# A graph network's setup on one core: the order in which x, the weights and the edge lists are loaded and used

## Chip, core and metric

The kernel runs on one core of one Trainium2 chip. The metric is the device time of one launch in microseconds. The kernel before takes 2194.6 us (median of three runs, 2194.39 to 2196.65).

## What is computed

A two-layer graph attention network over N = 3125 nodes of width 1024 and E = 50000 edges that are sorted by their target node. Each layer is added to its input and normalized. Only the first layer matters here, and of it only what stands ahead of its main products:

```python
xp = (x @ W).reshape(N, H, C)              # N=3125, H=4 heads, C=256, W is 1024 x 1024
a_src = jnp.einsum('nhc,hc->nh', xp, att_src)
a_dst = jnp.einsum('nhc,hc->nh', xp, att_dst)
e = jax.nn.leaky_relu(a_src[src] + a_dst[dst], 0.2)
ee = jnp.exp(e - m[dst])                   # m: the largest e of each target node
alpha = ee / z[dst]                        # z: the sum of ee of each target node
out = jax.ops.segment_sum(xp[src] * alpha[:, :, None], dst, num_segments=N)
x = _layernorm(x + relu(out + bias))       # then the second layer, in the same way
```

The kernel uses that `a_src` and `a_dst` are x times a small matrix, `wa` (1024 x 8): the weights W projected on the attention vectors.

## The kernel before

The change touches the setup, roughly the first 93 us. After it the kernel's first main stage multiplies the transposed x with W on TensorE (the line `L973` of the profile).

The setup is two blocks of hand-written programs, one for each engine, that meet at a barrier. The first block (`order_edges`) tests whether the edges are sorted, copies them, and already issues the loads of the attention vectors and of W (`load_weights`, eight parts of 128 rows, 512 KB each; three count on one semaphore, five on another). The second block has these programs:

- **SP** issues the loads of x. x is 25 tiles of 128 nodes, loaded as 13 pairs (1 MB each, the last is 53 rows). Before, it issues pairs 0 and 1, then one load of the last target of each chunk of 128 edges (`isrc`, 390 words of 4 bytes), then eleven small loads of the edge lists (`wrow` and `lrow`, up to 110 rows of about 512 bytes), and then the other pairs of x.
- **TensorE** transposes each tile of x (eight blocks of 128x128, counted by the profile as 8 or 16 instructions for one or two tiles), and ScalarE copies each tile back from PSUM to SBUF (`evict`). Tiles go in *quads*, quarters of x of four pairs each. When a quad's tiles are all transposed and `wa` is there, `products_a` multiplies the quad with `wa` (`L631`). `sources` transposes tables of the edge chain, `sums(0)` and `sums(1)` transpose the results of the first two and the last two quads (`L648`), and `first_tile` does the first products of the main stage (`L655`). `in_turn` holds this order for TensorE and ScalarE alike. Ahead of one tile TensorE broadcasts a row of 391 words (`s_bcast`) that VectorE's edge chain waits for.
- **VectorE** computes `wa` in eight steps, one for each part of W, each of eight `tensor_tensor_reduce` (the profile's `L692 CUSTOM_DVE_ANT_0` and the reading of its sum). Then comes the *edge chain* (`L701` to `L736`), which makes the table `ct`, the chunk numbers `cii`, and numbers for each block of edges. Then it waits for the gathered table `st` and derives `wrow`, `lrow` and the masks from it (`L746` to `L769`), and last the attention terms of the nodes (`L772` to `L783`).
- **GpSimd** stores `ct` to memory and gathers its rows as `st`.

Of the kernel before, what the change touches and what calls it, by code (L numbers as in the profile page):

```python
# [31 lines left out]
P = 128  # L32
# [276 lines left out]
def gnn_kernel(nc, x, src, dst, w0, att_s, att_d, bias, rms_w, w_down, wl, wr, att1, w_up, out):  # L309
# [22 lines left out]
    with top:  # L332
# [37 lines left out]
        with ExitStack() as ph:  # L370
# [12 lines left out]
            assert 5 * KEYS + EC <= (NT - 1) * D  # L383
# [124 lines left out]
            def in_turn(tile, quad, sources, sums):  # L508
                for t in range(14):
                    tile(t)  # L510
                quad(0)
                tile(14)
                tile(15)
                quad(1)
                for t in range(16, 24):
                    tile(t)
                sources()
                quad(2)
                sums(0)
                tile(24)  # L520
                quad(3)
# [6 lines left out]
            with nc.Block() as block:  # L528
                @block.gpsimd
                def _(pool):  # L530
                    pool.wait_ge(s_ct, 1)
# [10 lines left out]
                def _(sp):  # L542
                    sp.wait_ge(s_pad, 4)
                    load_x(sp, range(2))
                    with nc.allow_non_contiguous_dma(reason="one word of each chunk"):
                        sp.dma_start(lasti[0:1, 0:NCF], dst[0:NCF * P].rearrange("(c k) -> k c", k=P)[P - 1:P, :])\
                          .then_inc(s_lrow, 16)
                    dh = dst.tensor

                    first = sp.dma_start(dx[0:1, 0, 1:P + 2], dst[0:P + 1].rearrange("(a k) -> a k", a=1))  # L550
                    first.then_inc(s_edges, 16)
                    n_edge = 1
                    for b in range(NB):
                        c0, c1 = max(1, b * TB), min((b + 1) * TB, NCF)
                        sp.dma_start(dx[c0 - b * TB:c1 - b * TB, b, :],
                                     bass.AP(dh, c0 * P - 1, [[P, c1 - c0], [1, P + 2]])).then_inc(s_edges, 16)
                        c0 = b * TB
                        sp.dma_start(sx[0:c1 - c0, b, :],
                                     src[c0 * P:c1 * P].rearrange("(p k) -> p k", k=P)).then_inc(s_edges, 16)
                        n_edge += 2  # L560
                    pl, bl = NCF % TB, NCF // TB
                    sp.dma_start(dx[pl:pl + 1, bl, 0:E_LAST + 1],
                                 dst[NCF * P - 1:E].rearrange("(a k) -> a k", a=1)).then_inc(s_edges, 16)
                    sp.dma_start(sx[pl:pl + 1, bl, 0:E_LAST],
                                 src[NCF * P:E].rearrange("(a k) -> a k", a=1)).then_inc(s_edges, 16)
                    assert n_edge + 2 == N_EDGE_DMAS
                    load_x(sp, range(2, NPAIR))
# [9 lines left out]
                def _(act):  # L577
                    def evict(t):
                        act.wait_ge(s_tr, t + 1)
                        r = t % 2  # L580
# [3 lines left out]
                    def take_a(q):  # L584
                        act.wait_ge(s_am, q + 1)
                        n = min(2 * P, (NT - 2 * GROUPS * q) * P)
                        nc.scalar.activation(aT[:, q, 0:n], psum[:, 4 + 2 * (q % 2), 0:n], ACT.Copy).then_inc(s_ac, 1)
# [1710 lines left out]
```

## Time and profile before

| | |
|---|---|
| median of three runs | 2194.6 us |
| the profiled execution: its time, its span | 2195.57 us, 2193.9 us |
| TensorE busy over the span | 1793.3 us, 82% |
| VectorE busy | 1514.8 us, 69% |
| GpSimd, ScalarE busy | 1197.0 us (55%), 996.7 us (45%) |
| end of the setup (VectorE's first instruction of the next block) | 92.87 us |

All rows come from one profiled execution, with times counted from the start of its span. The setup is some 4% of the span (92.87 of 2193.9 us), so shares over the whole span say little about it; the timelines of its engines say more. A timeline row is a start, a duration, the engine, the line of the kernel, what is written from what, and in brackets how long the engine was idle ahead of it and what ended that.

### The profile page before, as it was taken

What the parts mean: (1) busy time and instruction counts of PE and PEld (TensorE: products, weight loads), DVE (VectorE), ACT (ScalarE), POOL (GpSimd) and SP (SyncE); (2) the same over time, 40 slices, a digit from 0 to 9 for tenths busy, and PEclk for the clock granted to TensorE, in tenths of its full rate; (3) what the DMA queues carried; (4) which work ended last, traced back from release to release, by engine and by line L of the source; (5) the groups of instructions that cost most, each with busy time, mean ns of one, the idle gap of its engine ahead of it and who ended that gap; (6) DMA issues with size and microseconds to landing.
All of it is one profiled execution on the core that took longest, in us unless ns stands there. A gap on an engine that the chain in (4) does not pass through costs nothing. (4 is left out here: it accounts for less than half of the span.)

```text
span 2193.9 us, 51575 instructions
## 1 busy us (share of the span) xinstructions
PE 1793.3 (82%) x12059; PEld 1230.1 (56%) x12060; DVE 1514.8 (69%) x3657; ACT 996.7 (45%) x3133; POOL 1197.0 (55%) x1696
## 2 busy tenths in 40 slices
PE   4899999995888888888849896887878878466688
PEld 3555555543666566566638774665666666455543
DVE  6577777747766666666669983555656556888867
ACT  3200000024777777777747662332333333466566
POOL 1122222223777777777711116777777776588780
PEclk9999999997999999999979998999999999699999
DMA  8345443313999999999999965887879877988757
GB/s 329 114 109 106 106 106 107 101 45 119 362 357 352 361 358 353 358 357 353 360 271 319 306 204 161 246 242 216 251 229 246 247 223 226 286 311 310 270 193 261
DMA packets 254648, 539.12 MB, mean 246 GB/s; under 512 B 40301, under 2 KB 146422, under 8 KB 254510
## 3 DMA queue, kind: packets, MB, share of 16 engines
q0 software_dynamic: 87696, 275.50, 36.5%
q1 hardware_dynamic: 72670, 175.70, 25.6%
q10 hardware_dynamic: 94176, 86.66, 13.7%
q8 instruction: 47, 0.77, 0.1%
q14 instruction: 59, 0.48, 0.1%
HBM read 448.51 MB, written 102.18 MB: 251 GB/s over the span
## 5 line engine op out<-in xcount | busy, mean ns | idle before, releaser
L1248 ACT ACTIVATE wone<-onehot,w 128x64 f32<-128x64 f32 x1760 | 432.3, 333 | 149.5 <-DVE onehot L1294 144.1
L161 POOL DMA_INDIRECT acc<-xl_table,csrc x392 | 395.0, 1008 | 128.0 <-issue 114.6
L1265 PE MATMUL banks<-w_sb,wone 128*64 128x256 f32 x2368 | 318.5, 395 | 77.6 <-DMA w_sb<-xp_table,isrc 46.8
L161 POOL DMA_INDIRECT w_sb<-xp_table,isrc x296 | 296.9, 1003 | 90.5 <-issue 57.0
L973 PE MATMUL banks<-w_sb,acc 128*128 128x512 f32 x736 | 342.5, 604 | 0.0
L1290 DVE TENSOR_TENSOR acc<-banks,acc 128x512 f32 x440 | 304.4, 692 | 0.0
L1737 PE MATMUL banks<-acc,onehot_t 128*128 x880 | 231.8, 408 | 82.5 <-ACT onehot_t L1712 56.9
L1765 DVE SCALAR_TENSOR_TENSOR prod<-banks,att_relu 128x1024 f32<-128x1024 f32 x110 | 134.7, 1225 | 205.7 <-ACT w L1702 205.7
L1737 PEld LDWEIGHTS banks<-acc,onehot_t 128*128 128x128 f32 x880 | 163.2, 195 | 146.2 <-issue 122.6
L1742 PE MATMUL banks<-acc,ident 128*128 x880 | 217.5, 391 | 24.6 <-POOL tabs L1664 24.5
L1265 PEld LDWEIGHTS banks<-w_sb,wone 128*64 128x64 f32 x2368 | 163.2, 138 | 127.1 <-issue 42.7
L1708 ACT ACTIVATE away<-lt,edge 128x512 f32<-128x512 bf16 x110 | 79.4, 722 | 296.8 <-issue 152.3
L1742 PEld LDWEIGHTS banks<-acc,ident 128*128 128x128 f32 x880 | 167.0, 193 | 64.0 <-issue 38.6
L973 PEld LDWEIGHTS banks<-w_sb,acc 128*128 128x128 f32 x736 | 131.2, 191 | 122.1 <-issue 122.0
L1289 DVE TENSOR_TENSOR zacc<-banks,zacc 64x9 f32 x440 | 69.8, 159 | 187.4 <-PE banks L1268 169.0
L863 POOL COPY w<-at_dst 128x16 f32 (+1 forms) x110 | 30.7, 279 | 308.0 <-DVE w L1071 268.0
L1878 POOL TENSOR_TENSOR scan_buf<-rows,w 128x1536 f32<-128x1536 f32 x55 | 151.7, 2777 | 49.6 <-PE banks L1918 32.5
L1918 PE MATMUL banks<-scan_buf 128*64 128x132 f32 x1760 | 126.4, 286 | 62.8 <-DVE acc L1947 33.4
L1265 PE MATMUL banks<-rows_c,wone 128*64 128x256 f32 x1152 | 153.4, 390 | 27.1 <-DMA rows_c<-xp_table,isrc 14.1
L161 POOL DMA_INDIRECT rows_c<-xp_table,isrc x144 | 144.3, 1002 | 43.9 <-issue 26.2
L909 ACT ACTIVATE zacc<-pidx 128x450 f32<-128x450 f32 x1 | 0.6, 577 | 361.9 <-DVE onehot_t L1059 361.9
L1268 PEld LDWEIGHTS banks<-w,onehot 128*64 128x64 f32 x880 | 121.3, 138 | 64.9 <-issue 1.9
(340 smaller groups left out, 2936.4 us busy)
## 6 DMA issues: line engine op xcount, KB each, us to landing
edge_rows<-acc ACTq DMA_DIRECT2D x440, 130.0 KB
rows<-edge_rows SPq DMA_DIRECT2D x55, 1040.0 KB, 5.0
lt_bc<-local_dst ACTq DMA_DIRECT2D x110, 128.0 KB, 3.6
lt<-local_dst SPq DMA_DIRECT2D x110, 128.0 KB, 4.3
w<-acc SPq DMA_DIRECT2D x100, 128.0 KB, 3.5
x_table<-y POOLq DMA_DIRECT2D x25, 512.0 KB, 5.9
acc<-x_table SPq DMA_DIRECT2D x25, 512.0 KB, 3.6
low_bc<-src_low ACTq DMA_DIRECT2D x98, 128.0 KB, 4.1
```

The costliest lines, as they stand in the source:

```text
L161: return self.pool.indirect_dma_start(out, None, table, bass.IndirectOffsetOnAxis(ap=idx, axis=0), bounds_check=self.bound, oob_is_err=False)
L973: last = nc.tensor.matmul(psum[:, 2 * r + i], xT_all[:, u, k, :], w_sb[:, k, i * 512:(i + 1) * 512], start=(k == 0), stop=(k == KD - 1))
L1248: last = nc.scalar.activation(wone[:, s, j, h, :], onehot[:, s, j, :], ACT.Copy, scale=w9[:, bass.ds(g * U + j, 1), h:h + 1].rearrange("p ...
L1265: nc.tensor.matmul(psum[WN * a:WN * (a + 1), j, k * C:(k + 1) * C], wone[:, s, j, h, :], slots[r][:, j, h * C:(h + 1) * C], start=True, st ...
L1268: nc.tensor.matmul(psum[0:WN, 4 + j, 0:W9], onehot[:, s, j, :], w9[:, bass.ds(i, 1), :].rearrange("p a n -> p (a n)"), start=True, stop=Tr ...
L1290: nc.vector.tensor_tensor(av, psum[:, j, :], av, ALU.add).then_inc(s_acc, 1)
L1708: nc.scalar.activation(away[:], lt[:, s].rearrange("p j e -> p (j e)"), ACT.Abs, bias=edge[:, 0:1]).then_inc(s_ab, 1)
L1737: nc.tensor.matmul(psum[:, 4 * s2 + j, 0:XRW], onehot_t[:, s2, j, :], xr[:, bass.ds(ds[j], 1), :].rearrange("p a n -> p (a n)"), start=Tru ...
L1742: last = nc.tensor.matmul(psum[:, 4 * s2 + j, 0:XLW], ident[:], rows[:, bass.ds(ss[j], 1), :].rearrange("p a n -> p (a n)"), start=False, ...
L1765: nc.vector.scalar_tensor_tensor(out=prod[:, s], in0=psum[:, 4 * s:4 * s + 4, 0:HID], scalar=0.0, in1=bc(att_relu[:].unsqueeze(1), [P, U, ...
L1878: nc.gpsimd.tensor_tensor(msg[:, s, :, 0:POOL_HEADS, 0:HD], rows[:, r, :, 0:POOL_HEADS * HD].rearrange("p j (h c) -> p j h c", c=HD), bc(w ...
L1918: last = nc.tensor.matmul(psum[WN * a:WN * (a + 1), bank, c:c + 2 * HS], onehot[:, u, first + j, :], msg[:, s, j, 2 * a:2 * a + 2, :].rear ...
```

## The change

Four things change, all in the setup:

1. The quads go in the order third, first, second, fourth (`QUAD_ORDER`), and the tiles with them (`TILE_ORDER`: 16 to 23, 0 to 15, 24). Pairs 8 and 9, half of the third quad, are loaded ahead of W, in `load_weights`; the other eleven loads of x follow in the second block without a break.
2. The load of `isrc` and the eleven edge loads are issued by GpSimd instead of SP, at the start of the second block.
3. VectorE does its edge chain between the third and the fourth part of W, and signals that `wa` is ready (`s_wa`) after the fifth to eighth.
4. TensorE transposes twenty tiles and does `sources` ahead of the first quad's products; the broadcast stands ahead of the ninth tile (`BCAST = 8`), not ahead of the eleventh.

```diff
-            assert 5 * KEYS + EC <= (NT - 1) * D
+            EARLY, BCAST = 2, 8
+            QUAD_ORDER = [EARLY, *(q for q in range(len(QUADS)) if q != EARLY)]
+            TILE_ORDER = [t for q in QUAD_ORDER for p in QUADS[q] for t in (2 * p, 2 * p + 1) if t < NT]
+            place_of = {t: i for i, t in enumerate(TILE_ORDER)}
+            turn_of = {q: i for i, q in enumerate(QUAD_ORDER)}
...
             def load_weights(sp):
                 sp.dma_start(attd, att_d.rearrange("h c -> (h c)").partition_broadcast(P)).then_inc(s_att, 16)
+                load_x(sp, QUADS[EARLY][:2])
                 for k in range(KD):
...
             def in_turn(tile, quad, sources, sums):
-                for t in range(14):
-                    tile(t)
-                quad(0)
-                tile(14)
-                tile(15)
-                quad(1)
-                for t in range(16, 24):
+                for t in TILE_ORDER[:20]:
                     tile(t)
                 sources()
-                quad(2)
+                quad(QUAD_ORDER[0])
+                for t in TILE_ORDER[20:24]:
+                    tile(t)
+                quad(QUAD_ORDER[1])
+                quad(QUAD_ORDER[2])
                 sums(0)
-                tile(24)
-                quad(3)
+                tile(TILE_ORDER[24])
+                quad(QUAD_ORDER[3])
                 sums(1)
...
                 @block.gpsimd
                 def _(pool):
+                    pool.wait_ge(s_pad, 4)
+                        pool.dma_start(lasti[0:1, 0:NCF], dst[0:NCF * P].rearrange("(c k) -> k c", k=P)[P - 1:P, :])\
+                          .then_inc(s_lrow, 16)
...
+                    for b in range(NB):
+                        c0, c1 = max(1, b * TB), min((b + 1) * TB, NCF)
+                        pool.dma_start(dx[c0 - b * TB:c1 - b * TB, b, :],
+                                     bass.AP(dh, c0 * P - 1, [[P, c1 - c0], [1, P + 2]])).then_inc(s_edges, 16)
...
                     pool.wait_ge(s_ct, 1)
...
                 @block.sync
                 def _(sp):
                     sp.wait_ge(s_pad, 4)
-                    load_x(sp, range(2))
...
-                        sp.dma_start(lasti[0:1, 0:NCF], dst[0:NCF * P].rearrange("(c k) -> k c", k=P)[P - 1:P, :])\
-                          .then_inc(s_lrow, 16)
...
-                    load_x(sp, range(2, NPAIR))
+                    load_x(sp, [p for q in QUAD_ORDER for p in QUADS[q]][2:])
...
                     def transposes(t):
                         pe.wait_ge(s_xi[t // 2], 16)
-                        wait(pe, s_xT, t - 1)
-                        if t == 10:
+                        i = place_of[t]
+                        wait(pe, s_xT, i - 1)
+                        if i == BCAST:
                             pe.wait_ge(s_lastw, 1)
...
                     def sums(i):
                         pe.wait_ge(s_csrc, 1)
-                        pe.wait_ge(s_ac, min(2 * i + 2, len(QUADS)))
+                        pe.wait_ge(s_ac, 1 + max(turn_of[2 * i], turn_of[2 * i + 1]))
...
                 @block.vector
-                    for k in range(KD):
+                    def project(k):
                         dve.wait_ge(s_w[k >= W_FIRST], 16 * (KD - W_FIRST if k >= W_FIRST else W_FIRST))
-                        if k == W_FIRST:
-                            dve.wait_ge(s_iota, 11)
-                            dve.wait_ge(s_lrow, 16)
-                            link(nc.vector.tensor_copy(lastf, lasti))
-                            nc.vector.tensor_tensor(lastw, lastf, iotc, ALU.add).then_inc(s_lastw, 1)
...
-                    nc.vector.tensor_copy(mark0[:], pidx[:]).then_inc(s_wa, 1)
+                    for k in range(W_FIRST):
+                        project(k)
+                    dve.wait_ge(s_iota, 11)
+                    dve.wait_ge(s_lrow, 16)
+                    link(nc.vector.tensor_copy(lastf, lasti))
+                    nc.vector.tensor_tensor(lastw, lastf, iotc, ALU.add).then_inc(s_lastw, 1)
 
                     dve.wait_ge(s_edges, 16 * N_EDGE_DMAS)
                     link(nc.vector.tensor_copy(dxf, dx))
...
                     link(nc.vector.scalar_tensor_tensor(out=toff[:], in0=toff[:], scalar=float(WN), in1=dneg[:],
                                                         op0=ALU.mult, op1=ALU.add))
+
+                    for k in range(W_FIRST, KD):
+                        project(k)
+                    nc.vector.tensor_copy(mark0[:], pidx[:]).then_inc(s_wa, 1)
```

The program of TensorE from its first transpose of the setup, before (`acc` is x, `nt` is `wa`, `isfirst` is the row that is broadcast, `ct` and `val` are the edge tables of `sources`):

```order
L618 MATMUL banks<-ident,acc 128x128 x80
L615 MATMUL banks<-isfirst,any_b 110x391
L618 MATMUL banks<-ident,acc 128x128 x32
L631 MATMUL banks<-acc,nt 32x256 x32
L618 MATMUL banks<-ident,acc 128x128 x16
L631 MATMUL banks<-acc,nt 32x256 x32
L618 MATMUL banks<-ident,acc 128x128 x64
L639 MATMUL banks<-ident,ct 128x110
```

And now:

```order
L623 MATMUL banks<-ident,acc 128x128 x64
L620 MATMUL banks<-isfirst,any_b 110x391
L623 MATMUL banks<-ident,acc 128x128 x96
L644 MATMUL banks<-ident,ct 128x110
L645 MATMUL banks<-ident,val 128x110
```

Both quads' products that stood ahead of `sources` have left this piece; twenty tiles (160 transposes) stand there.

The same engine from the last transpose of `sources` on, before (the `w` of `L648` holds the quads' products):

```order
L640 MATMUL banks<-ident,val 128x110
L631 MATMUL banks<-acc,nt 32x256 x32
L648 MATMUL banks<-ident,w 128x128 x4
L618 MATMUL banks<-ident,acc 128x128 x8
L631 MATMUL banks<-acc,nt 32x128 x8
L648 MATMUL banks<-ident,w 128x128 x3
L655 MATMUL banks<-w_sb,acc 128x512 x4
```

And now:

```order
L645 MATMUL banks<-ident,val 128x110
L636 MATMUL banks<-acc,nt 32x256 x32
L623 MATMUL banks<-ident,acc 128x128 x32
L636 MATMUL banks<-acc,nt 32x256 x64
L653 MATMUL banks<-ident,w 128x128 x4
L623 MATMUL banks<-ident,acc 128x128 x8
L636 MATMUL banks<-acc,nt 32x128 x8
L653 MATMUL banks<-ident,w 128x128 x3
L660 MATMUL banks<-w_sb,acc 128x512 x4
```

Four tiles and two quads' products have come in between the first quad and `sums(0)`; from `sums(0)` on the rows are as they were.

VectorE at the end of `wa`, before (`ISA` is `tensor_tensor_reduce` and the reading of its sum, `w` the attention vectors):

```order
L692 ISA w,nt<-w_sb,w 128x256
L692 ISA nt 128x1
L698 COPY mark<-pidx 128x1
L701 CAST st<-wrow 110x520
L702 CAST ct<-lrow 110x4x128
```

And now:

```order
L692 ISA w,nt<-w_sb,w 128x256
L692 ISA nt 128x1
L746 COPY mark<-pidx 128x1
L749 COPY chi<-banks 128x392
L750 CAST csrc<-banks 128x440
```

`L746` is what releases the quads' products; the edge chain (`L706` to `L741` now) has left its place behind it and stands ahead of the last 40 projections.

## Rows read from the trace of the kernel before

**Rows 1.** Busy time by stretch of the setup; the columns are named in its first line.
```profile
core 0: us, PE busy (x) PEld busy (x) DVE busy (x) ACT busy (x) POOL busy (x), PEclk, DMA share, GB/s
16.00:25.00 9.00, 0.00 (x0) 0.00 (x0) 8.44 (x46) 1.09 (x1) 0.00 (x0) 1.00 1.03 411
25.00:32.50 7.50, 5.25 (x25) 5.09 (x26) 2.08 (x9) 2.05 (x2) 0.00 (x0) 1.00 0.62 168
32.50:55.00 22.50, 18.07 (x191) 13.93 (x193) 21.81 (x95) 13.96 (x15) 1.10 (x1) 1.00 1.03 411
...
84.00:87.00 3.00, 3.00 (x7) 1.45 (x6) 2.69 (x10) 0.96 (x2) 0.00 (x0) 0.50 0.00 0
...
100.00:110.00 10.00, 10.00 (x67) 5.29 (x66) 6.92 (x16) 0.00 (x0) 1.73 (x10) 1.00 0.56 159
```

**Rows 2.** Timeline of the SP queue: start, duration, line, transfer, count.
```profile
15.80 0.92 SPq L468 DMA_DIRECT2D acc<-in_x  x2
...
18.50 7.69 SPq L558 DMA_DIRECT2D lrow<-src_ordered  x1
...
29.51 12.28 SPq L468 DMA_DIRECT2D acc<-in_x  x10
```

**Rows 3.** Timeline of TensorE, 30 to 90 us; idle time before and releaser in brackets.
```profile
34.62 1.97 PE L618 MATMUL banks<-ident,acc 128*128 128x128 f32 x16 [1.16 <-DMA acc<-in_x]
...
39.73 1.97 PE L618 MATMUL banks<-ident,acc 128*128 128x128 f32 x16 [0.59 <-DMA acc<-in_x]
...
57.65 1.97 PE L618 MATMUL banks<-ident,acc 128*128 128x128 f32 x16
59.94 1.98 PE L618 MATMUL banks<-ident,acc 128*128 128x128 f32 x16 [0.33 <-ACT acc L581]
...
67.58 3.66 PE L631 MATMUL banks<-acc,nt 128*32 128x256 f32 x64 [0.36 <-ACT acc L581]
71.17 0.65 PE L648 MATMUL banks<-ident,w 128*128 128x128 f32 x4
...
76.56 3.60 PE L655 MATMUL banks<-w_sb,acc 128*128 128x512 f32 x8
82.35 0.57 PE L664 MATMUL banks<-ident,lrow 110*128 110x110 f32 x4 [2.19 <-DVE ab L767]
...
84.16 5.02 PE L655 MATMUL banks<-w_sb,acc 128*128 128x512 f32 x8
89.02 0.54 PE L670 MATMUL banks<-ident,af 110*4 110x110 f32 x4
```

**Rows 4.** Timeline of VectorE in the setup.
```profile
16.58 0.42 DVE L692 CUSTOM_DVE_ANT_0 w<-w_sb,w 128x256 f32<-128x256 f32 x1 [0.38 <-DMA w_sb<-in_L_gnn_W]
...
30.97 0.35 DVE L687 CAST wdst<-isrc 1x391 f32<-1x391 int32 x1 [5.39 <-DMA isrc<-dst_ordered]
...
31.84 0.41 DVE L692 CUSTOM_DVE_ANT_0 w<-w_sb,w 128x256 f32<-128x256 f32 x1
...
46.88 0.15 DVE L698 COPY mark<-pidx 128x1 f32<-128x1 f32 x1
...
49.29 0.62 DVE L709 TENSOR_SCALAR ldst<-banks,step 110x391 f32<-110x391 f32 x1
...
59.83 0.16 DVE L736 SCALAR_TENSOR_TENSOR toff<-toff,dneg 110x4 f32<-110x4 f32 x1
...
92.87 0.57 DVE L1050 COPY w<-isfirst 128x440 f32<-128x440 f32 x1 [0.29 <-PEq L528]
```

**Rows 5.** Timeline of GpSimd: the issues of its DMAs.
```profile
49.69 1.10 POOL L532 DMA_DIRECT2D edge_table<-ct  x1 [40.84 <-DVE ct L705]
...
63.14 1.07 POOL L161 DMA_INDIRECT st<-edge_table,cii  x1 [0.30 <-issue]
```

**Rows 6.** DMAs issued before 140 us: from issue to landing in us, at the row's end.
```profile
edge_table<-ct POOLq DMA_DIRECT2D x1, 880.0 KB, 11.1
...
st<-edge_table,cii POOLq DMA_INDIRECT x4, 4.1
```

More of the change, by code:

```diff
@@ L530, in _ @@
                 def _(pool):
+                    pool.wait_ge(s_pad, 4)
+                    with nc.allow_non_contiguous_dma(reason="one word of each chunk"):
+                        pool.dma_start(lasti[0:1, 0:NCF], dst[0:NCF * P].rearrange("(c k) -> k c", k=P)[P - 1:P, :])\
+                          .then_inc(s_lrow, 16)
+                    dh = dst.tensor
+                    first = pool.dma_start(dx[0:1, 0, 1:P + 2], dst[0:P + 1].rearrange("(a k) -> a k", a=1))
+                    first.then_inc(s_edges, 16)
+                    n_edge = 1
+                    for b in range(NB):
+                        c0, c1 = max(1, b * TB), min((b + 1) * TB, NCF)
+                        pool.dma_start(dx[c0 - b * TB:c1 - b * TB, b, :],
+                                     bass.AP(dh, c0 * P - 1, [[P, c1 - c0], [1, P + 2]])).then_inc(s_edges, 16)
+                        c0 = b * TB
+                        pool.dma_start(sx[0:c1 - c0, b, :],
+                                     src[c0 * P:c1 * P].rearrange("(p k) -> p k", k=P)).then_inc(s_edges, 16)
+                        n_edge += 2
+                    pl, bl = NCF % TB, NCF // TB
+                    pool.dma_start(dx[pl:pl + 1, bl, 0:E_LAST + 1],
+                                 dst[NCF * P - 1:E].rearrange("(a k) -> a k", a=1)).then_inc(s_edges, 16)
+                    pool.dma_start(sx[pl:pl + 1, bl, 0:E_LAST],
+                                 src[NCF * P:E].rearrange("(a k) -> a k", a=1)).then_inc(s_edges, 16)
+                    assert n_edge + 2 == N_EDGE_DMAS
                     pool.wait_ge(s_ct, 1)
@@ L543, in _ @@
                     sp.wait_ge(s_pad, 4)
-                    load_x(sp, range(2))
-                    with nc.allow_non_contiguous_dma(reason="one word of each chunk"):
-                        sp.dma_start(lasti[0:1, 0:NCF], dst[0:NCF * P].rearrange("(c k) -> k c", k=P)[P - 1:P, :])\
-                          .then_inc(s_lrow, 16)
[L548 to L566, printed above, removed]
-                    load_x(sp, range(2, NPAIR))
+                    load_x(sp, [p for q in QUAD_ORDER for p in QUADS[q]][2:])
                     sp.wait_ge(s_low, 1)
@@ L617, in transposes @@
                         for k in range(KD):
-                            last = nc.tensor.transpose(psum[:, 2 * (t % 2) + k // 4, (k % 4) * P:(k % 4 + 1) * P],
+                            last = nc.tensor.transpose(psum[:, 2 * (i % 2) + k // 4, (k % 4) * P:(k % 4 + 1) * P],
                                                        acc[:, t, k * P:(k + 1) * P], ident[:])
@@ L622, in products_a @@
                     def products_a(q):
-                        if q == 0:
+                        if q == QUAD_ORDER[0]:
                             pe.wait_ge(s_wa, 1)
-                        tiles = min(2 * QUADS[q][-1] + 2, NT)
-                        pe.wait_ge(s_xT, tiles)
-                        wait(pe, s_ac, q - 1)
+                        last_tile = min(2 * QUADS[q][-1] + 1, NT - 1)
+                        pe.wait_ge(s_xT, place_of[last_tile] + 1)
+                        wait(pe, s_ac, turn_of[q] - 1)
                         for k in range(KD):
@@ L630, in products_a @@
                                 n = min(2, NT - 2 * p)
-                                last = nc.tensor.matmul(psum[COLS * j:COLS * (j + 1), 4 + 2 * (q % 2), 0:n * P], wa[:, k, :],
+                                last = nc.tensor.matmul(psum[COLS * j:COLS * (j + 1), 4 + 2 * (turn_of[q] % 2), 0:n * P], wa[:, k, :],
                                                         xT_all[:, 2 * p:2 * p + n, k, :], start=(k == 0), stop=(k == KD - 1))
```

9 lines of the change are left out of this document (5 added, 4 removed).

## The prediction

> **What bounds the setup now.** I read the timelines of the setup's engines against each other, then the windows. The reader is to see three spans of work that end one after the other.
>
> The first is the DMA. From 16 to 25 us the engines move 411 GB/s and are full, from 25 to 32.5 us only 168 GB/s, and from 32.5 to 55 us 411 again [rows 1]. In the hole SP stands in the issue of one edge load for 7.7 us and comes to the third pair of x only at 29.5 [rows 2]. TensorE gets the third pair at 34.6 and the fifth at 39.7; it could have transposed before [rows 3].
>
> The second is VectorE. It begins on W at 16.6, waits 5.4 us for `isrc`, has `wa` ready at 47.0 and the edge chain at 60.0 [rows 4].
>
> The third is the end. TensorE comes to `first_tile` at 76.6 with all quads done, then stands 2.2 us until VectorE's masks are there at 82.35, works to about 90.7, and the next block begins at 92.87 [rows 3, 4]. So the edge chain, with the store and the gather behind it, ends last, and the quads have some 2 us of air. From 100 us on TensorE is busy 10.0 of 10 us [rows 1]: what the setup's end moves, the kernel's end moves too, one for one.
>
> **The weights come later.** Two pairs (2.1 MB) now stand ahead of W in the same queue. At 411 GB/s [rows 1] that is 5.1 us. VectorE's first projection began at 16.58, released by a part of W [rows 4], so it now begins at 21.7. SP's two more issues take 0.92 us [rows 2] and lie inside the wait for that landing.
>
> **VectorE's row of work.** Nothing in it becomes shorter. The first three parts take 9.0 us (16.58 to where it begins to wait for `isrc`, 30.97 - 5.39 = 25.58), `lastf` and `lastw` 0.9, the five last parts 15.0 (31.84 to 46.88), the copies and comparisons ahead of the broadcast row 2.4 (46.88 to 49.29), the rest of the edge chain 10.7 (49.29 to 59.99) [rows 4]. Together 38.0. Its first 9.9 us end at 31.6. From there it waits for two things.
>
> - *The edge loads.* GpSimd issues twelve DMAs. Its issues of a table of 110 rows take 1.07 to 1.10 us with 0.30 between two: 1.37 each [rows 5]. Twelve from 15.8 on begin their last at 30.9. From issue to landing the nearest rows are 4.1 us for a gather and 11.1 for the 880 KB store that had x beside it [rows 6]. Bounds 35.0 and 42.0. I take 36, near the gather, since each load is small (some 55 KB), with a little for the company of x. The comparisons then end at 38.4 (37.4 to 44.4).
> - *The broadcast row.* It stands ahead of the ninth tile, which waits for the fifth pair to land. That was 39.7 [rows 3]. The same W and pairs are ahead of it now, but the hole is filled: 7.5 us at 168 instead of 411 GB/s are 1.8 MB, 4.4 us. So 35.3 to 39.7, and as the edge loads now share the engines I take the middle, 37.5, and 0.5 for the broadcast: 38.0.
>
> So the counting that needs both begins at 38.4 (from 35.8, where the edges are prompt too, to 44.4). Behind it 10.7 and 15.0 and the mark: `wa` is ready 25.8 us later, at 64.2 instead of 47.0. Behind that signal all quads' products wait, in TensorE's program and so also the four tiles behind the first quad.
>
> **TensorE from `wa` to the end.** Ahead of it all is hidden: twenty tiles are transposed soon after their pairs land, at about 54, since ten pairs at the old spacing (39.7 - 34.6 = 5.1 us for two) end near 52 us [rows 3]. Then it stands some 10 us. From `wa` on: the first quad 3.6, four tiles 4.3 (2.29 for the pair at 57.65 and 1.97), two more quads 7.2 (3.59 each, 67.58 to 71.17), 0.5 and the start 0.2 for ScalarE's copy ahead of `sums(0)` (its waits here are 0.33 to 0.36): 15.8. From `sums(0)` to `first_tile` the rows are those of before: 5.4 (71.17 to 76.56). Then 3.6, the masks' transposes 1.8 (82.35 to 84.16), the second part of `first_tile` 3.6, and 3.85 to the next block (89.02 to 92.87) [rows 3, 4]. Together 34.0.
>
> **The clock.** The second part of `first_tile` took 5.02 us where the first took 3.60; the granted clock was 0.50 from 84 to 87 (1.2 GHz), after TensorE had stood 2.2 us [rows 1, 3]. With the masks long there this stand is gone, so I took 3.6 above. But the stand of 10 us now precedes the first quad: I add the same 1.4. `first_tile` itself is where the gain of 1.4 shows.
>
> **The sum.** 64.2 + 34.0 + 1.4 = 99.6, against 92.87: 6.7 us later. What was on the path, the masks, is no longer: the chain ends at about 49, the store and gather lie under the last projections, and from the chain's end to the masks VectorE took 22.4 us with all waits (59.99 to 82.35) [rows 3, 4]; from 64.2 that is 86.6 at most, and TensorE wants them at 64.2 + 24.8 = 89. The profiled execution took 2195.57, so 2202.3; the median of the runs lies 1.0 below it, so 2201.3. Least: 35.8 + 25.8 + 34.0 = 95.6, no clock lost, +2.7, 2197.3. Most: 44.4 + 25.8 + 35.4 = 105.6, +12.7, 2207.3.
>
> **A page against it.** The Trainium skill, page "DMA: Bandwidth & Descriptors", section "Issuing engines are not separate DMA queues", says that DMAs started by different engines run on the same 16 DMA engines, and that starting them from several saves only the time on the issuing sequencer. The trace has a case in which that time is much: the 12.8 us from the end of SP's two first x issues to the third pair [rows 2]. By the page alone the edge loads still take their room from x and the fifth pair comes at 39.7 rather than 37.5; that would put the counting at 40.2 and the end 1.8 us later.
>
> **Rivals.**
> - *Not slower: the weights are not delayed.* If the two pairs found room that the DMA engines leave unused before 16 us, VectorE would start at 16.6, and without another wait its 38.0 us would end at 54.6; then 54.6 + 35.4 = 90.0, 2.9 us faster, 2191.7. It decides from `wa` at 57.5. Against it: that also needs the edges and the fifth pair by about 29, and these are 35 at the earliest. 4%.
> - *The setup's end is hidden, or nothing is delayed that matters:* within 0.2%, 2194.6. For it, the main stage has other waits further on; against it, TensorE's 10.0 of 10 us [rows 1]. 8%.
> - *The edge loads crawl.* One of them has 109 rows, and the issue behind it took 7.7 us on SP [rows 2]. If its rows all go to one DMA engine, each in turn with a 4 KB row of x (0.16 us at 411 GB/s over 16), that is 109 x 0.19 = 21 us, and the other loads' share behind it some 13: the edges would be there at about 52, not 36. 52 + 2.4 + 25.8 + 35.4 = 115.6: 22.7 slower, 2217.3. The page's section "Queues, rings and completion order" says that a DMA engine takes its queues in turn by packets, which may hold several rows; by that the price is smaller. 8%.
> - *The forecast:* 80%, between 2197.3 and 2207.3.
>
> **How the numbers follow.** Of the forecast's 80% the part within 0.2% (4.4 us, about what a measurement of this kernel can tell from no change) is that below +4.4: some 12 in 100. So slower 76%, same 20%, faster 4%. The range is the forecast's own, taken a little further down for a clock that costs nothing: 2196.5 to 2207.5, and the other three cases are left out.
>
> **What the profile of the changed kernel would show.** The first projection at 21 to 22 us; DMA at over 400 GB/s from 16 to 50 us without a hole; the counting (`L714`) from 38; `cii` at 44; the mark (`L746`) at 64; TensorE idle from about 54 to then, and its first quad's products slow; the masks ready ahead of the last quad; the next block at 99 to 100. The prediction is wrong if VectorE starts on W at 17 us, if the edges are not there at 42, or if the next stage begins at 99 and the kernel yet ends at 2195.

## Result, and the profile after

The changed kernel takes 2201.82 us (median of 13 runs, 2199.37 to 2205.11), the kernel before 2195.69 (median of 13, 2192.63 to 2199.10). The ratio is 1.0029, with a 95% interval of 1.0021 to 1.0036: 6.1 us slower. Its profiled execution took 2205.11 us, the longest of the 13; its span is 2203.4 us with a mean granted clock of 0.954, against 2193.9 and 0.964 before.

The stretches of the setup that stand in [rows 1], now:

```profile
core 0: us, PE busy (x) PEld busy (x) DVE busy (x) ACT busy (x) POOL busy (x), PEclk, DMA share, GB/s
16.00:25.00 9.00, 5.89 (x31) 5.65 (x29) 1.29 (x7) 4.45 (x5) 6.45 (x12) 0.97 1.04 334
25.00:32.50 7.50, 0.00 (x0) 0.00 (x0) 7.33 (x41) 0.00 (x0) 0.00 (x0) 0.50 1.03 383
32.50:55.00 22.50, 17.02 (x109) 15.22 (x110) 16.06 (x48) 12.06 (x13) 5.85 (x5) 0.80 1.03 402
84.00:87.00 3.00, 2.38 (x30) 1.55 (x20) 0.00 (x0) 0.85 (x5) 0.00 (x0) 1.00 0.00 0
```

The hole in the DMA from 25 to 32.5 us is filled, 383 GB/s for 168. But from 16 to 25 the rate is 334 for 411, with the engines just as full (a share of 1.04). And TensorE's low clock, which was there from 84 to 87 us, is now at the front of the setup.

VectorE, beside [rows 4]:

```profile
23.71 0.43 DVE L692 CUSTOM_DVE_ANT_0 w<-w_sb,w 128x256 f32<-128x256 f32 x1 [8.24 <-DMA w_sb<-in_L_gnn_W]
...
32.74 0.35 DVE L702 CAST wdst<-isrc 1x391 f32<-1x391 int32 x1
...
33.61 0.41 DVE L706 CAST st<-wrow 110x520 f32<-110x520 int32 x1
...
41.49 0.63 DVE L714 TENSOR_SCALAR ldst<-banks,step 110x391 f32<-110x391 f32 x1 [5.47 <-PE banks L620]
...
52.27 0.16 DVE L741 SCALAR_TENSOR_TENSOR toff<-toff,dneg 110x4 f32<-110x4 f32 x1
...
67.51 0.15 DVE L746 COPY mark<-pidx 128x1 f32<-128x1 f32 x1
...
81.86 0.17 DVE L776 COPY ab<-val 110x16 f32<-110x16 f32 x1
```

VectorE works from 23.71 without a wait: the casts of `isrc` and of the edges show no idle time in brackets. The one wait inside its row of work is 5.47 us for the broadcast row. Then chain, five parts and mark follow without a gap that matters, and the masks are done at 82.0.

TensorE, beside [rows 3]:

```profile
15.45 6.44 PE L623 MATMUL banks<-ident,acc 128*128 128x128 f32 x32 [7.14 <-DMA acc<-in_x]
34.71 4.51 PE L623 MATMUL banks<-ident,acc 128*128 128x128 f32 x24 [12.82 <-DMA acc<-in_x]
39.55 1.06 PE L623 MATMUL banks<-ident,acc 128*128 128x128 f32 x8 [0.33 <-ACT acc L585]
40.55 0.90 PE L620 MATMUL banks<-isfirst,any_b 1*110 1x391 f32 x2
...
58.29 3.37 PE L623 MATMUL banks<-ident,acc 128*128 128x128 f32 x16 [2.57 <-DMA acc<-in_x]
...
67.72 5.90 PE L636 MATMUL banks<-acc,nt 128*32 128x256 f32 x64 [5.04 <-DVE mark L746]
...
90.83 3.60 PE L660 MATMUL banks<-w_sb,acc 128*128 128x512 f32 x8
...
95.78 3.61 PE L660 MATMUL banks<-w_sb,acc 128*128 128x512 f32 x8
...
103.09 8.77 PE L993 MATMUL banks<-w_sb,acc 128*128 128x512 f32 x16 [2.19 <-PEq L532]
```

TensorE transposes the first two pairs early, then stands 12.82 us for the third, which is there at 34.71 (34.62 before). It then begins at half clock: the 32 transposes of two pairs and the gaps between them take from 34.71 to 40.55, 5.8 us, where a pair at full clock takes 1.97 and 0.3. The granted clock (the third value from the right) in this stretch:

```profile
35.00:37.50 2.50, 2.50 (x13) 2.50 (x12) 1.02 (x2) 0.78 (x1) 0.93 (x1) 0.50 1.02 406
37.50:40.00 2.50, 2.17 (x17) 1.96 (x16) 0.00 (x0) 1.86 (x3) 0.00 (x0) 0.86 1.03 413
```

The broadcast row stands behind these two pairs and behind the landing of the fifth. The issue of the fifth pair by SP, and how long it took from issue to landing (the last value):

```profile
18.58 3.87 SPq L474 DMA_DIRECT2D acc<-in_x  x1
...
acc<-in_x SPq DMA_DIRECT2D x1, 1024.0 KB, 21.2
```

It landed at 18.58 + 21.2 = 39.8. Before, it was issued at 30.49, took 9.2 and landed at 39.7. So the row, which begins at 40.55, waited for the landing until 39.8 and some 0.8 us more for TensorE.

The first quad takes 5.90 us after a stand of 5.04, where one took 3.66 before. The second half of `first_tile` takes 3.61, not 5.02. The next block begins at 103.09 instead of 92.87, 10.2 later.

GpSimd's issues (line, transfer, count), beside [rows 5]:

```profile
15.60 0.88 POOL L537 DMA_DIRECT2D isrc<-dst_ordered  x1 [6.91 <-POOLq L204]
...
21.91 0.53 POOL L555 DMA_DIRECT2D lrow<-src_ordered  x1
36.32 0.93 POOL L559 DMA_DIRECT2D edge_table<-ct  x1 [13.87 <-DVE ct L710]
```

Twelve issues end at 22.44, 0.51 to 0.58 us each behind the first. How long such loads took from issue to landing stands in the last column of the DMA view, beside [rows 6]:

```profile
lrow<-src_ordered POOLq DMA_DIRECT2D x3, 55.0 KB, 6.8
...
isrc<-dst_ordered POOLq DMA_DIRECT2D x1, 1.5 KB, 7.2
...
lrow<-src_ordered POOLq DMA_DIRECT2D x1, 0.3 KB, 6.4
```

**From the setup to the whole kernel.** The setup is 10.2 us longer, the kernel 6.1. The first instruction of the gather stage and the first of the stage behind it show where the rest goes; before:

```profile
526.38 0.43 DVE L1294 TENSOR_TENSOR onehot<-iotar,wdst 128x256 f32<-128x256 f32 x1 [1.92 <-PEq L853]
...
1112.27 0.64 PE L1478 MATMUL banks<-zacc,ident 128*64 128x225 f32 x4 [1.34 <-PEq L1225]
```

After:

```profile
537.22 0.42 DVE L1303 TENSOR_TENSOR onehot<-iotar,wdst 128x256 f32<-128x256 f32 x1 [2.21 <-PEq L862]
...
1118.48 0.63 PE L1487 MATMUL banks<-zacc,ident 128*64 128x225 f32 x4 [1.34 <-PEq L1234]
```

From the end of the setup to the gather stage: 526.38 - 92.87 = 433.5 us before and 537.22 - 103.09 = 434.1 after. TensorE is full there (busy 290.0 of the 290 us from 110 to 400 in both kernels) and passes the delay on one for one. The gather stage itself: 585.9 before, 581.3 after, 4.6 shorter. 10.2 + 0.6 - 4.6 = 6.2, what the medians show. The stages behind 1112 and 1118 us took 3.3 longer in this profiled execution (1084.9 of span for 1081.6), which is what it lies above the median.

### The profile page after: what moved, and what is told of

Same layout as the page of the kernel before. It is cut to its first block and busy times, and to the rows that moved or that the text cites. A ratio compares the mean times of both kernels' runs of the same rounds, so it can differ in the third digit from the quotient of the medians.

```text
span 2203.4 us, 51574 instructions
## 1 busy us (share of the span) xinstructions
PE 1802.7 (82%) x12059; PEld 1242.8 (56%) x12060; DVE 1515.4 (69%) x3657; ACT 997.0 (45%) x3133; POOL 1199.2 (54%) x1708
## 5 line engine op out<-in xcount | busy, mean ns | idle before, releaser
L161 POOL DMA_INDIRECT acc<-xl_table,csrc x392 | 392.9, 1002 | 127.6 <-issue 111.4
```

The source lines that it names most:

```text
L161: return self.pool.indirect_dma_start(out, None, table, bass.IndirectOffsetOnAxis(ap=idx, axis=0), bounds_check=self.bound, oob_is_err=False)
```

## The experiments

The kernels ran on two kinds of chip. On one, the kernel before takes about 2194 us, on the other 2536 to 2554. There the gather stage takes 717 to 733 us, varying by more than is at stake. The setup's end agrees between the two kinds within 0.1 to 1.2 us for the three kernels that were profiled on both; the largest difference between two executions of one kernel is 2.4 us (runs 8 and 11). So on the second kind I read where the setup ends, and rest nothing on ratios of whole kernels. Runs 1 to 8, 11 and 12 fell on the second kind, 9 and 10 on the first. The theory: VectorE's row of work behind late weights, held further by the broadcast row, sets `wa`, and `wa` the end. The rival after the result: something else (the weights alone, the DMA of the edges, the clock) sets it.

**1. The broadcast earlier.** The broadcast row ahead of the fifth tile and ahead of its wait for x, otherwise the changed kernel.

```diff
-            EARLY, BCAST = 2, 8
+            EARLY, BCAST = 2, 4
...
-                        pe.wait_ge(s_xi[t // 2], 16)
                         i = place_of[t]
-                        wait(pe, s_xT, i - 1)
                         if i == BCAST:
...
+                        pe.wait_ge(s_xi[t // 2], 16)
+                        wait(pe, s_xT, i - 1)
```

> The changed kernel with one edit: TensorE sends the broadcast row ahead of the fifth tile and ahead of the wait for that tile's x, not ahead of the ninth behind the wait for the fifth pair. In the changed kernel VectorE waited 5.5 us (36.0 to 41.5) for this broadcast. Theory (the broadcast is what VectorE waits for last, and all behind it is one row of work): the counting starts at 36 instead of 41.5, wa is ready at 62 instead of 67.5, the next block begins at 97.7 instead of 103.1, and the kernel is 5.4 us faster than the changed one, about 2196. Rival (the weights behind two pairs of x are what delays the end, and the wait is only room they leave): under 1 us, 2202.

The next block begins at 96.72, 6.4 us before that of the changed kernel:

```profile
33.74 1.64 PE L618 MATMUL banks<-isfirst,any_b 1*110 1x391 f32 x2 [12.79 <-DVE isfirst L703]
...
63.60 3.66 PE L636 MATMUL banks<-acc,nt 128*32 128x256 f32 x64
...
96.72 8.79 PE L993 MATMUL banks<-w_sb,acc 128*128 128x512 f32 x16 [2.19 <-PEq L532]
```

The broadcast now waits for VectorE and not the other way round. The mark comes at 61.72 instead of 67.51, 5.8 earlier. The first quad begins only at 63.60, since the transposes of `sources` stand ahead of it, but at full clock: 4.1 us of the 6.4 are the earlier start, 2.2 the clock. Ratio to before 1.0030 (1.0005 to 1.0056). The wait for the broadcast row was on the path.

**2. The weights first.** The changed kernel without the two pairs ahead of W.

```diff
-                load_x(sp, QUADS[EARLY][:2])
...
-                    load_x(sp, [p for q in QUAD_ORDER for p in QUADS[q]][2:])
+                    load_x(sp, [p for q in QUAD_ORDER for p in QUADS[q]])
```

> The changed kernel with one edit: no pair of x ahead of W; all 13 loads of x are issued in the second block, in the changed order of quads. Theory: VectorE begins on W at 16.6 instead of 23.7, but the broadcast still stands behind the fifth pair, which has the same bytes ahead of it, so the counting starts at 40 to 41 as in the changed kernel and the next block begins at 101.5 to 103; 0 to 1.5 us faster than the changed kernel. Rival (the lateness of the weights passes through to the end): 7.1 us faster, the next block at 96, 2195.

The first projection begins at 16.27, 7.4 us earlier, and the next block at 103.97, 0.9 later. VectorE waits 11.45 us for the broadcast row instead of 5.47 and counts at 43.15:

```profile
29.57 6.25 PE L622 MATMUL banks<-ident,acc 128*128 128x128 f32 x32 [21.23 <-DMA acc<-in_x]
...
42.21 0.90 PE L619 MATMUL banks<-isfirst,any_b 1*110 1x391 f32 x2 [1.83 <-DMA acc<-in_x]
...
69.37 5.13 PE L635 MATMUL banks<-acc,nt 128*32 128x256 f32 x64 [9.41 <-DVE mark L745]
```

So the late weights, in the changed kernel, cost nothing: the broadcast row, which waits for the fifth pair, was later than they were. The edit moves more than the weights: the fifth pair too now lands some 2.4 us later (the row begins at 42.21, just behind it), which is why the end came 0.9 us later where 0 to 1.5 us earlier was expected. Ratio 1.0062 (1.0038 to 1.0086).

**3. Both.** The weights first, as in 2, and the broadcast ahead of the first tile.

> The changed kernel with both edits: W ahead of all x, and the broadcast ahead of the first tile. Neither wait is left: VectorE has its first projection at 16.6, lastf and lastw at 26.5, the edge loads are there at 28.3 as in the changed kernel, the counting starts at 31, wa is ready at 56.8, the next block begins 35.4 later, at 92.2. Theory (VectorE's row of work in front of wa plus TensorE's 35.4 behind it make the time): about that of the kernel before, -0.7 us. Rival (TensorE's tail grows, because it then also waits for x or its clock is lower): 95 or more.

The mark came at 58.12, but the next block only at 99.04, where 92.2 was expected: the theory missed here, and the rival (TensorE also waits for x, or its clock is lower; 95 or more) held. The rows of TensorE say why:

```profile
43.89 4.47 PE L622 MATMUL banks<-ident,acc 128*128 128x128 f32 x24 [2.83 <-DMA acc<-in_x]
...
53.96 3.58 PE L622 MATMUL banks<-ident,acc 128*128 128x128 f32 x16 [1.93 <-DMA acc<-in_x]
...
59.77 5.46 PE L622 MATMUL banks<-ident,acc 128*128 128x128 f32 x32 [2.23 <-DMA acc<-in_x]
...
65.91 3.66 PE L635 MATMUL banks<-acc,nt 128*32 128x256 f32 x64
```

The new order has a third limit: twenty tiles and `sources` stand ahead of the first quad. They end at 65.9, with waits for x and half clock on the way. With `wa` 7.8 us before that, the tiles decide. Ratio 1.0032 (1.0011 to 1.0053).

**4 and 6. GpSimd alone.** The kernel before, with nothing changed but the twelve small loads, moved from SP to GpSimd. Twice.

```diff
                 def _(pool):
+                    pool.wait_ge(s_pad, 4)
+                    with nc.allow_non_contiguous_dma(reason="one word of each chunk"):
+                        pool.dma_start(lasti[0:1, 0:NCF], dst[0:NCF * P].rearrange("(c k) -> k c", k=P)[P - 1:P, :])\
+                          .then_inc(s_lrow, 16)
...
                 def _(sp):
                     sp.wait_ge(s_pad, 4)
                     load_x(sp, range(2))
-                    with nc.allow_non_contiguous_dma(reason="one word of each chunk"):
-                        sp.dma_start(lasti[0:1, 0:NCF], dst[0:NCF * P].rearrange("(c k) -> k c", k=P)[P - 1:P, :])\
-                          .then_inc(s_lrow, 16)
...
```

> The kernel before with one part of the change: the twelve edge loads issued by GpSimd; order of x, of VectorE and of TensorE as before. VectorE no longer stands 5.4 us for isrc, so wa is ready at 41.6 and the edge chain ends at 54.6 instead of 60.0. Theory (in both kernels VectorE stood until about 72.3 for the store of src_low, which queues behind the last load of x): that wait stays at 72, the masks at 82.3, the next block at 92.9: no change, within 0.5 us. Rival (the edge chain's end is what sets the masks): 5.4 us faster, next block at 87.5 to 89.5.

> The kernel before with only the edge loads moved to GpSimd, once more, for its time and for its setup's end. There its next block began at 89.56, 3.3 us earlier than in the kernel before. Theory (the setup's end moves the kernel's end one for one): 3.3 us faster than the kernel before, 0.15%, within an interval of about that size; next block at 89.6. Rival (the end was luck of one execution): next block at 92 to 93.

The next block begins at 89.56 and 90.02, 3.3 and 2.9 us before that of the kernel before. VectorE has `wa` at 41.07 instead of 46.88. It still stands ahead of its first step on the gathered table, by the profile for the store of `src_low`, but till 70.15 instead of 72.30, so the masks come 2.1 us earlier. TensorE stands only 0.28 us for them instead of 2.19, and the second half of `first_tile` runs at full clock (3.61 us for 5.02). Neither of the two answers put down for run 4 has 89.56 in it: the wait did not stay at 72, and the earlier `wa` did not pass through whole. The ratios are 0.9993 (0.9967 to 1.0018) and 0.9988 (0.9967 to 1.0009): undecided on this kind of chip.

**5. The changed kernel again,** on the slower kind of chip.

> The changed kernel once more. Its profiled execution had the next block at 103.1 us, 10.2 later than the kernel before, while the medians of the two kernels stood only 6.1 us apart. If the setup is the same in each execution, the next block begins within 0.5 us of 103.1 here, and the difference between 10.2 and 6.1 lies in the stages behind it. If the setup itself varies (what the DMA engines do, TensorE's clock), it begins elsewhere, between 98 and 104.

First projection 23.46, counting 42.65, mark 68.64, next block 103.39, against 103.09: the setup repeats within 0.3 us at its end. In between it does not repeat as well: the mark came 1.1 us later, and the clock on the first quad cost 0.8 us less (5.07 for 5.90). Ratio 1.0026 (1.0007 to 1.0044).

**7. The old order.** The changed kernel with VectorE's five last parts ahead of the edge chain again, and TensorE's products of the quads back where they stood; the loads ahead of W and GpSimd stay.

```diff
-                for t in TILE_ORDER[:20]:
+                for t in TILE_ORDER[:14]:
                     tile(t)
-                sources()
                 quad(QUAD_ORDER[0])
...
+                    for k in range(W_FIRST, KD):
+                        project(k)
+                    nc.vector.tensor_copy(mark0[:], pidx[:]).then_inc(s_wa, 1)
...
-                    for k in range(W_FIRST, KD):
-                        project(k)
-                    nc.vector.tensor_copy(mark0[:], pidx[:]).then_inc(s_wa, 1)
```

> The changed kernel with its orders undone: VectorE does all eight parts of W and signals wa before the edge chain, and TensorE and ScalarE have the quads' products where the kernel before had them (the third quad takes the first's place). Two pairs ahead of W and the edge loads by GpSimd stay. Theory (the late wa with all quads behind it is what costs, and neither the loads' order nor GpSimd does): wa at 23.7 + 9.0 + 0.9 + 15.0 = 48.6, the edge chain to 61.7, the store and the gather to about 72, the masks at 82, next block at 91 to 93, 10 us earlier than the changed kernel. Rival (weights that come 7 us later cost that at the end in any order): next block at 97 or later.

```profile
48.31 3.66 PE L638 MATMUL banks<-acc,nt 128*32 128x256 f32 x64
...
90.62 8.80 PE L994 MATMUL banks<-w_sb,acc 128*128 128x512 f32 x16 [2.19 <-PEq L534]
```

The first quad runs at 48.31 instead of 67.72, and the next block begins at 90.62, 12.5 us before that of the changed kernel and 2.3 before that of before. This splits the 10.2: GpSimd's loads -3.4 (89.46 in run 9, for 92.87), the two pairs ahead of W with the new order of x and the broadcast's new place +1.2 (90.62 for 89.46, no more than two executions can differ by), the new order of VectorE and TensorE +12.5. The order is the cost. More than half of it is the broadcast row, which in the old order VectorE does not wait for: with the new order kept, moving that row alone brings 6.4 us (run 1) and 7.5 (run 10). The ratio is 0.9942 (0.9922 to 0.9962, four runs), some 15 us; the setup explains 2.3 of them, and the rest stands on the kind of chip whose later stages vary.

**8 and 11. The edge loads back on SP,** in the changed kernel. Twice.

```diff
-                        pool.dma_start(lasti[0:1, 0:NCF], dst[0:NCF * P].rearrange("(c k) -> k c", k=P)[P - 1:P, :])\
+                        sp.dma_start(lasti[0:1, 0:NCF], dst[0:NCF * P].rearrange("(c k) -> k c", k=P)[P - 1:P, :])\
...
```

> The changed kernel with one edit: the twelve edge loads are issued by SP again, at the start of the second block, ahead of the other eleven loads of x. Theory (GpSimd's small loads took turns with W on the DMA engines and so delayed it): the first projection begins 2 us earlier than in the changed kernel, at 21.7 instead of 23.7; the counting still waits for the broadcast behind the fifth pair, at 40 to 42, so the next block begins at 101 to 104. Rival (the two pairs alone take 7 us): first projection at 23.7 as before.

> The changed kernel with the edge loads on SP again, as in the experiment before, for its time. In three kernels whose edge loads GpSimd issues, the gather stage behind the main products took 580.6 to 581.3 us between its barriers, and 585.9 in the kernel before; that is where 4 of the changed kernel's 10 us come back. Theory (twelve more DMAs on GpSimd's queue are what shortens that stage): without them it takes 585 to 586 on a chip on which the kernel before takes 2195 us, the next block begins at 100.6, and the kernel is 7.7 us slower than before, a ratio of 1.0035. Rival (the stage is shorter by the new order of the setup, or by luck of single executions): 581, a ratio of 1.0015.

The first projection begins at 21.45 and 21.63, 2.1 to 2.3 us before the changed kernel's 23.71. From 16 to 25 us the rate is 411 and 409 GB/s again, and the hole is back (201 and 222 from 25 to 32.5). So the two pairs delay W by the 5 us forecast, and GpSimd's loads by 2 more. The counting came at 41.30 and 41.07, hardly earlier than 41.49: the third pair was at 33.85 and 33.72. The ends differ, 100.64 and 103.06, where 101 to 104 and 100.6 were expected. The first quad of run 8:

```profile
67.52 3.66 PE L635 MATMUL banks<-acc,nt 128*32 128x256 f32 x64 [1.50 <-DVE mark L745]
```

And that of run 11:

```profile
67.10 6.50 PE L635 MATMUL banks<-acc,nt 128*32 128x256 f32 x64 [3.37 <-DVE mark L745]
```

The same kernel, a stand of 1.50 us in one and 3.37 in the other, and 2.8 us of clock between them: less the 0.4 us by which run 11's quad begins earlier, that is the whole difference of the ends. Run 8's quad ran at full clock (1.00 from 66.5 to 71), run 11's at half (0.50 from 67.1 to 72.8). Ahead of it TensorE had run at half clock in both, on the last pair of the twenty tiles (0.50 from 61 to 64.5, and from 59.5 to 62.6). Ratios 1.0053 (1.0035 to 1.0072) and 1.0027 (1.0008 to 1.0046).

**9. GpSimd alone, on the kind of chip of the first runs.** The kernel of 4 and 6.

> The kernel before with only the edge loads moved to GpSimd, for its time: its next block began 3.3 and 2.9 us earlier in two executions. Theory (the setup's end moves the kernel's end one for one): 3 us faster, a ratio of 0.9986 on a chip on which the kernel before takes 2195 us. Rival (a later stage takes it back): 1.000.

2186.91 us (median of 6) for 2193.42 (median of 16): ratio 0.9967 (0.9955 to 0.9980), faster than both kernels of this case. The next block and the next two stages begin at:

```profile
89.46 10.10 PE L985 MATMUL banks<-w_sb,acc 128*128 128x512 f32 x16 [2.19 <-PEq L528]
...
524.20 0.43 DVE L1295 TENSOR_TENSOR onehot<-iotar,wdst 128x256 f32<-128x256 f32 x1 [2.21 <-PEq L854]
...
1104.84 0.64 PE L1479 MATMUL banks<-zacc,ident 128*64 128x225 f32 x4 [1.34 <-PEq L1226]
```

3.4 us are won in the setup, and the gather stage is again shorter, 580.6 us for 585.9. The Trainium skill, page "DMA: Bandwidth & Descriptors", section "Issuing engines are not separate DMA queues", says that starting DMAs from several engines saves only the time on the sequencer, which is usually small beside the DMA. The trace agrees on what is saved: from 16.72 to 29.51 SP did nothing but issue these loads [rows 2]. Here that time is not small, and saving it brings 3.4 us of setup.

**10. The broadcast earlier, on the same kind of chip.** The kernel of 1.

> The changed kernel with the broadcast sent early, as in the first experiment, for its time and once more for its setup's end, which was 96.7, 3.8 us behind the kernel before. Theory: next block at 96.7 again, 3.8 us slower than the kernel before, a ratio of 1.0017; the changed kernel had 1.0029 with its next block at 103.1. Rival (the setup's end counts for less than one for one): 1.001 or less.

2193.30 us, ratio 0.9999 (0.9990 to 1.0008):

```profile
95.55 8.77 PE L993 MATMUL banks<-w_sb,acc 128*128 128x512 f32 x16 [2.19 <-PEq L532]
```

The next block begins 2.7 us after that of before, and 1.2 earlier than in run 1. The gather stage runs from 529.68 to 1110.71, 581.0 us. The theory (3.8 us slower) missed, and the rival, 1.001 or less, held. With the broadcast in another place the change as a whole costs nothing that can be measured. But it gains nothing either: against run 9, which has GpSimd's loads and none of the rest, the setup's end is 6.1 us later and the kernel 6.4 us slower.

**12. Loads that nobody needs.** The kernel before, with twelve copies of the small loads by GpSimd into a buffer that is overwritten later. GpSimd (ahead of storing `ct`) and VectorE (ahead of the edge chain) wait for them; the computation is unchanged. It asks whether GpSimd's loads by themselves shorten the gather stage.

```diff
+                    first = pool.dma_start(spare_d[0:1, 0, 1:P + 2], dst[0:P + 1].rearrange("(a k) -> a k", a=1))
+                    first.then_inc(s_spare, 16)
...
```

> The kernel before, with the same twelve loads issued by GpSimd in addition at the start of the second block, into memory that is not in use yet; SP keeps its own. Nothing else moves, and no result uses the added loads. Theory (twelve more DMAs on GpSimd's queue, whatever they carry, shorten the gather stage behind): setup's end 93 to 95, since the loads take room from W and x; the gather stage 581 instead of 586; the kernel 2 to 4 us faster than before, 0.9985. Rival (the loads' place on SP is what costs): 586, and the kernel as before or up to 2 us slower.

It fell on the slower kind of chip, where that stage took 719.8 us and run 11's, without GpSimd's loads, 717.4, in a spread of 717 to 733: undecided. Ratio 1.0007 (0.9992 to 1.0023). The setup became 2.8 us longer (95.64).

**What the traces say of the gather stage.** The stage's length varies too much on the second kind of chip, but the time that GpSimd itself takes there does not. It issues 440 gathers in the stage; 296 of them go to `w_sb`. After the first bar stand their busy time in us and the mean of one in ns; before:

```profile
L161 POOL DMA_INDIRECT w_sb<-xp_table,isrc x296 | 296.9, 1003 | 90.5 <-issue 57.0 <-PE banks L1268 33.6
```

The changed kernel, and then run 8, which is the changed kernel with the edge loads on SP:

```profile
L161 POOL DMA_INDIRECT w_sb<-xp_table,isrc x296 | 294.3, 994 | 90.0 <-issue 45.3 <-PE banks L1277 44.8
...
L161 POOL DMA_INDIRECT w_sb<-xp_table,isrc x296 | 297.2, 1004 | 185.8 <-PE banks L1276 106.7 <-issue 69.9 <-DMA w_sb<-in_L_gnn_W 9.2
```

In the three traces in which SP alone loads the edges (before, 8, 11) one takes 1002 to 1004 ns, in the ten in which GpSimd does (after, 1 to 7, 9, 10) 993 to 997, in run 12 999. So the shorter issue goes with GpSimd's loads and not with the new order, which runs 8 and 11 have; in run 12, where SP and GpSimd both load the edges, it lies between. With the other 144 gathers that is 3.5 to 4.5 us on the first kind of chip (441.2 us before; 437.7, 436.7 and 436.9 now and in runs 9 and 10), where the stage is 4.6 to 5.3 us shorter. Why an issue is 5 to 11 ns shorter hundreds of us after those loads is open, and so is whether the stage follows it one for one, since GpSimd also waits for TensorE there.

## Why the prediction was right, point by point

The direction and the size of the total were right, 2201.3 for 2201.82. That they agree within 0.5 us is luck: two errors cancel, for the setup grew by 10.2 us and not 6.7, and some 4 us came back behind it. The mechanism was right in its main line (late `wa`, all quads behind it, TensorE's work behind that) and wrong in which wait ends last ahead of the counting.

- **The weights come later:** 5.1 us forecast, 7.1 measured (23.71). Runs 8 and 11 give the term without GpSimd's loads, 4.9 and 5.1: the two pairs were sized rightly, and the company of the small loads was left out. It also made the forecast's "over 400 GB/s from 16 to 50 us" wrong (334 from 16 to 25). On the path it made nothing in the changed kernel: VectorE stood 5.47 us for the broadcast row behind it.
- **VectorE's row of work:** right in every term, within 0.3 us: 9.0, 0.9, 2.4 (33.61 to where it begins to wait, 41.49 - 5.47 = 36.0), 10.9 and 15.1.
- **The edge loads:** mis-sized. 1.37 an issue and landed at 36 was taken; it was 0.51 to 0.58 and at 21.91 + 6.4 = 28.3 (the last issue and its time to landing). The forecast's 38.4 for the counting came from this term, by 0.4 us ahead of the broadcast row. In the run it was on no path: VectorE came to these loads only at 33.61 and did not wait. The rival of crawling loads is out.
- **The broadcast row:** this is the step that failed. Its end was forecast at 38.0 and was at 41.45. Of the 3.4 us, 2.3 are the landing of the fifth pair: the forecast took 37.5, the middle between the filled hole (35.3) and the old time (39.7), and it landed at 39.8. The hole was filled and no pair came earlier. Between 16 and 34.6 us the engines moved 6.72 MB for 5.84 before, yet the third pair landed no earlier; which transfers the rest belonged to the trace doesn't say, so why is open. Another 0.8 is TensorE, which the forecast reckoned at nothing: after 12.8 us of standing it transposed the third and fourth pair at first at half clock and was done with them only after the fifth had landed. The last 0.4 is the row itself, 0.90 for 0.5. The counting came 3.1 us later than forecast, the mark 3.3. The prediction's paragraph "A page against it" had the fifth pair at 39.7 and the counting at 40.2, nearer than the forecast's own numbers; that the room which the edge loads take is the reason, no run shows, for in runs 8 and 11, where SP issues them, the row came hardly earlier.
- **The hole:** the reading that SP stands in one edge load's issue "in the hole" is not quite what [rows 2] show. That issue ends at 26.19. In the hole, from 25 to 32.5, SP issues the eight small loads behind it up to 29.51, and then x. Nothing in the sum hangs on this.
- **TensorE's twenty tiles:** forecast to be done at 54, done at 61.7; the last of the ten pairs was waited for until 58.29, where the old spacing gave 52. Hidden behind the mark in the changed kernel, but in run 3 they set the end.
- **TensorE from `wa` on:** 35.4 forecast, 103.09 - 67.51 = 35.6 measured. The clock's share was 2.2 on the first quad, not 1.4, the small terms together 0.6 less, and the gain in the second half of `first_tile` came as forecast.
- **The masks off the path:** right, done at 82.0 and wanted at 94.3.
- **One for one to the kernel's end:** right for the next stage (433.5 and 434.1), wrong for the gather stage, 4.6 shorter. It was 581.3, 580.6 and 581.0 us in the three kernels in which GpSimd loads the edges, and 585.9 in the one profile of before on this kind of chip. The medians agree with that: run 9 is 6.5 us faster with 3.4 in the setup, run 10 equal with 2.7 more. GpSimd's own time there is 3.5 to 4.5 us shorter with its loads and not without them, so the loads are the likely cause. Why they would act there is open, and two more profiles of before on that chip would be needed to know the spread of the 585.9.
- **"The weights are not delayed"** and **"the setup's end is hidden"** are out: 23.71, and 434.1 us of full TensorE behind it.

## What to carry to other kernels

Before a long piece of work is moved behind another on one engine, list what the other engines have queued behind its signal: here `wa` came 20.6 us later and took all quads' products and four tiles with it; the new order as a whole cost 12.5 us of the setup. A one-instruction product that another engine waits for belongs ahead of waits for bulk data, not behind them (6.4 and 7.5 us of these 12.5 for moving it). And where one change bundles several edits, run each alone: the smallest one, small loads off the queue that carries the bulk loads, was worth 6.5 us by itself (run 9), and what run 10 has besides it cost 6.4.

## What the runs showed of the chip that was not expected

- Small direct loads issued by GpSimd cost 0.51 to 0.58 us of its time each behind the first (0.88), about half of what its gathers of edge rows take in the kernel before (1.06 to 1.11, and 0.30 between two).
- Those loads beside the bulk loads keep the DMA engines full and lower their yield: 334 GB/s at a share of 1.04 from 16 to 25 us, where the same stretch has 411 at 1.03 without them.
- Filling a hole of 7.5 us in the DMA did not bring the next pair of x forward (34.71 for 34.62, and 33.85 in run 8, where the hole remained).
- With those loads issued by GpSimd in the setup, its gathers hundreds of us later take 993 to 997 ns each, without them 1002 to 1004.
- The granted clock falls to 0.50 (1.2 GHz) while TensorE stands (0.50 from 25 to 32.5 us in the changed kernel, with TensorE idle), and the price falls on what runs next: a quad of 3.66 us took 5.90 after 5.04 us of standing, 6.50 after 3.37, 5.07 after 4.75 and 5.13 after 9.41, and 3.66 after 1.50, where the clock was back at 1.00 ahead of it. In these five rows the price doesn't grow with the stand.
